# A decoder layer on one core: the first tile's output-weight rounding, gathers and mask loads moved, and 17 products of zeros added

## The reference

```python
x = layernorm(x + self_attn(x))           # 32 query heads, 8 key/value heads, width 16, causal, rotary
x = layernorm(x + cross_attn(x, ctx))     # 32 query heads, 8 key/value heads, width 128, mask, rotary at pos
x = layernorm(x + ffn(x))                 # x @ W.T + bias, kept where a cluster test says so

def self_attn(x):
    q, k, v = rope(x @ Wq), rope(x @ Wk), x @ Wv
    p = softmax(where(causal, q @ k.T / 4, -inf))
    return (p @ v) @ Wo
```

## Time and profile before

| what | value |
|---|---|
| median of 3 runs | 819.03 us (818.23 to 821.03) |
| profiled execution | 817.94 us |
| its span, first to last instruction | 816.0 us |
| PE, DVE, ACT, POOL busy | 758.6, 607.5, 317.6, 392.2 us |
| mean granted clock of TensorE | 0.989 |

### The profile page before, as it was taken

One profiled execution on the slowest core, in us unless ns is written; L12 is line 12 of the kernel. 1 busy time (PEld: TensorE's weight loads), 2 busy tenths in 40 slices (PEclk: granted clock), 3 DMA queues, 4 the chain that ended last, 5 costly groups with the idle time before them and its releaser, 6 DMA issues.

```text
span 816.0 us, 13861 instructions
## 1 busy us (share of the span) xinstructions
PE 758.6 (93%) x4800; PEld 649.0 (80%) x4800; DVE 607.5 (74%) x1165; ACT 317.6 (39%) x669; POOL 392.2 (48%) x369
## 2 busy tenths in 40 slices
PE   4689999989999999999999999999999999989984
PEld 3577777779878887888888888888888888877763
DVE  4778888877787676676677768677766776788767
ACT  4455555562433323343333334324233333333313
POOL 7566666664545544453544445444444644442102
PEclk9899999999999999999999999999999999999998
DMA  9500004012343232222232222242222232120002
GB/s 264 118 18 17 16 16 119 3 55 53 81 127 79 64 81 79 62 53 51 78 77 77 77 51 51 53 103 75 51 77 51 55 78 75 46 85 1 1 0 103
DMA packets 107875, 53.53 MB, mean 66 GB/s; under 512 B 80449, under 2 KB 96961, under 8 KB 107841
## 3 DMA queue, kind: packets, MB, share of 16 engines
q1 hardware_dynamic: 107008, 51.51, 24.7%
q10 hardware_dynamic: 576, 1.05, 0.4%
q0 software_dynamic: 256, 0.52, 0.2%
HBM read 32.62 MB, written 2.10 MB: 43 GB/s over the span
## 4 chain that ended last, share of the span: by engine, by line
PE 64%; DVE 19%; issue 6%; POOL 4%; ACT 2%; DMA 2%; SPq 2%; DVEq 0%; ACTq 0%; POOLq 0%
PE bank L723 17%; PE bank L658 17%; PE bank L484 10%; DVE arena_r L1512 5%; PE s_bank L737 3%; PE bank L534 2%; PE s_bank L739 2%; PE bank L707 2%; PE bank L558 2%; DVE small L1600 2%; DVE arena_f L1594 1%; PE s_bank L707 1%; ACT arena_r L979 1%; PE s_bank L558 1%; DMA arena_f<-in_L_attn_Wo 1%
## 5 line engine op out<-in xcount | busy, mean ns | idle before, releaser
L723 PE MATMUL bank<-arena_r 128*128 128x512 f32 x768 | 192.2, 399 | 0.9 <-DVE arena_r L1512 0.9
L979 ACT ACTIVATE arena_r<-bank 128x256 fp32r<-128x256 f32 (+2 forms) x249 | 105.1, 458 | 222.6 <-PE bank L690 88.6
L658 PE MATMUL bank<-arena_r 128*128 128x512 f32 x720 | 185.2, 400 | 2.2 <-POOL arena_r L1396 1.6
L723 PEld LDWEIGHTS bank<-arena_r 128*128 128x128 f32 x768 | 139.9, 189 | 28.2 <-DVE arena_r L1512 1.3
L658 PEld LDWEIGHTS bank<-arena_r 128*128 128x128 f32 x720 | 130.7, 188 | 31.5 <-POOL arena_r L1396 2.1
L484 PE MATMUL bank<-arena_r 128*128 128x256 f32 (+1 forms) x1056 | 146.7, 295 | 1.5 <-DVE arena_r L1512 0.6
L484 PEld LDWEIGHTS bank<-arena_r 128*128 128x128 f32 x1056 | 137.4, 191 | 9.0 <-DVE arena_r L1512 1.5
L1512 DVE TENSOR_TENSOR arena_r<-bank,arena_r 128x256 fp32r<-128x256 f32 (+2 forms) x217 | 99.9, 486 | 58.5 <-ACT arena_r L979 57.9
L979 ACT ACTIVATE arena_r<-arena_f 128x512 fp32r<-128x512 f32 (+2 forms) x178 | 104.4, 637 | 61.6 <-DMA arena_f<-arena_f 47.7
L1512 DVE TENSOR_TENSOR arena_r<-arena_f,arena_r 128x512 fp32r<-128x512 f32 (+1 forms) x100 | 92.9, 937 | 17.6 <-ACT arena_r L979 17.5
L1387 POOL TENSOR_TENSOR arena_f<-arena_f 128x512 f32<-128x512 f32 x30 | 39.2, 1306 | 114.2 <-DVE arena_f L1681 114.2
(11 more groups left out here) (153 smaller groups left out, 1169.9 us busy)
## 6 DMA issues: line engine op xcount, KB each, us to landing
arena_f<-arena_f SPq DMA_DIRECT2D x120, 128.0 KB, 2.5
arena_f<-in_L_xattn_Wo SPq DMA_DIRECT2D x8, 1024.0 KB, 5.6
arena_f<-in_L_xattn_Wq SPq DMA_DIRECT2D x14, 512.0 KB, 4.1
arena_f<-in_x SPq DMA_DIRECT2D x8, 256.0 KB, 2.8
arena_f<-in_x SPq DMA_DIRECT2D x1, 2048.0 KB, 15.5
arena_f<-in_L_xattn_Wk SPq DMA_DIRECT2D x8, 256.0 KB, 3.1
arena_f<-in_L_xattn_Wv SPq DMA_DIRECT2D x8, 256.0 KB, 3.3
arena_f<-in_ctx SPq DMA_DIRECT2D x8, 256.0 KB, 3.1
```

The lines of the kernel that those rows point to most:

```text
L658: mm = pe.matmul(BQ2[f][:], w2q_s[a][:, e, j, f, :], xT[b][:, e, tok], start=(e == 0 and n == 0), stop=(e == EC - 1 and n == 2))
L723: mm = pe.matmul(BO2[i][:], at2[a][:, h, i * P:(i + 1) * P], w2o_s[b][:, h, :], start=(h == 0 and n == 0), stop=(h == HG - 1 and n == 2))
L979: act.activation(dst, src, ACT.Copy).then_inc(done, 1)
```

## The change

Five edits. On SP, `next_x(1)` goes ahead of the W1o loads, and the two mask loads go behind `next_x(2)` and behind the four table copies. On ACT, the four roundings of W1o go from the start to tile 0, behind the last copy of `qk_stage(0)` and ahead of `expo(0, 0)`. On DVE, the four low pieces go from tile 0 to tile 1, two ahead of `masked_max(1, 1)` and two ahead of `masked_max(1, 3)`. On POOL, three of the eight gathers go behind the first tile's L1359. On PE, 17 products of a zeroed buffer into an unused bank are added: 5 ahead of `a_stage(0)`, 4 behind it, 8 ahead of `qk_stage(0)`; nothing reads them.

```diff
+            next_x(1)
             w1o_v = w1o.rearrange("(g h d) n -> g d h n", g=G1, h=HG)
             for g in range(G1):
                 sp.dma_start(w1out_raw[D1 * g:D1 * g + D1, :, :], w1o_v[g]).then_inc(d_w1o, 16)
-            next_x(1)
             sp.dma_start(res, x.rearrange("(t p) n -> p t n", p=P)).then_inc(d_res, 16)
-            for i in range(2):
+            def load_mask(i):
...
             next_x(2)
+            load_mask(0)
             sp.wait_ge(r_table, 2)
...
+            load_mask(1)
...
+            def warm(n):
+                for _ in range(n):
+                    pe.matmul(BO[:], vpad[0][:, 0, 0:P], vpad[0][:, 0, 0:512], start=True, stop=True)
...
+                if start:
+                    warm(8)
                 qk_stage(i, start)
...
+            pe.wait_ge(s_init, 1)
+            warm(5)
             pe.wait_ge(d_ident, 16)
             a_stage(0)
+            warm(4)
...
-            act.wait_ge(d_w1o, 16 * G1)
-            for h in range(HG):
-                copy(w1out[0][:, h, :], w1out_raw[:, h, :], s_w1oh)
...
                 if old:
                     at_high(v, not oldest)
+                else:
+                    act.wait_ge(d_w1o, 16 * G1)
+                    for h in range(HG):
+                        copy(w1out[0][:, h, :], w1out_raw[:, h, :], s_w1oh)
                 expo(i, 0)
...
-            for t in range(T):
+            for t in range(T - 3):
                 gather_rope(t)
...
+                if not old:
+                    for t in range(T - 3, T):
+                        gather_rope(t)
...
-                if not old:
-                    for h in range(HG):
-                        dve.wait_ge(s_w1oh, h + 1)
-                        low(w1out[1][:, h, :], w1out_raw[:, h, :], w1out[0][:, h, :], s_w1ol)
...
+                elif old:
+                    w1out_low(0)
+                    w1out_low(1)
                 masked_max(i, 1, not old)
...
+                elif old:
+                    w1out_low(2)
+                    w1out_low(3)
```

More of the change, by code:

```diff
@@ L1602, in total, with w1out_low @@
                 dve.reciprocal(sm1[u], sm1[u]).then_inc(s_rc, 1)
+            def w1out_low(h):
+                dve.wait_ge(s_w1oh, h + 1)
+                low(w1out[1][:, h, :], w1out_raw[:, h, :], w1out[0][:, h, :], s_w1ol)
             def tile_steps(i):
```

## The result

The changed kernel takes 826.79 us (median of 9 runs, 822.98 to 829.86) against 819.36 for the kernel before (9 runs). The ratio is 1.0088, 95% interval 1.0069 to 1.0107: slower by 7.4 us, 5.7 to 8.8. The direction was forecast; the size was not (823.7, range to 826.0), and the measured time lies outside the range. The profiled execution has a span of 824.1 us, 8.1 above the one before.

The account below looks back on a forecast made before the run. It took a chain through DVE's low pieces and `q_low` in tile 0, then `at_low(0)`, `wo_stage(0)`, `b_stage(2)` in tile 1, to bound the kernel. -5.9 + 1.8 + 7.0 + 1.8 = +4.7 us on 819.03 gave 823.7, range 818.3 to 826.0.

Parts of the forecast that it names:

- What bounds it, and the sign: Tile 1: `at_low(0)`, `wo_stage(0)`, `b_stage(2)` follow without a gap, PE has no slack; slower given 0.60.
- Gain of tile 0: Tile 0: `qk_stage(0)` starts at 18.3, not 22.75, and `masked_max(0, 0)` at 22.6, not 28.52; gain 5.9 us.
- The gathers' wait: Tile 0: `table_turn` on PE waits for three late gathers, landing at 26.3; cost 1.8 us, bounds 0.8 and 3.6.
- the prediction's own rule: Tile 0: for no cost, `table_turn` must start by 24.5, early enough for `masked_max(0, 2)` 4.15 us after the first.
- The stand of `wo_stage(0)`: Tile 1: PE waits for DVE's last low pieces, slowed by POOL; cost 7.0 us, bounds 4.8 and 7.4.
- Its clock: Tile 1: PE's half clock behind the wait slows `wo_stage(0)` and `b_stage(2)`; cost 1.8 us, bounds 0 and 2.3.
- The sum: Whole kernel: -5.9 + 1.8 + 7.0 + 1.8 = +4.7 us, span 820.7, median 823.7.
- Rival 3: Tile 0: gathers land at 28.1, or half clock takes 1.4 off the gain; +6.1 to +6.5, about 825.3; chance 0.11.
- The loads of x and the masks, ACT's roundings: Moved loads on SP and W1o roundings on ACT cost nothing; 0.5 if ACT were late by one rounding.
- The signs: Profile: `qk_stage(0)` near 18.3 at clock 1.0, `table_turn` waits 2 to 4 us, `wo_stage(0)` 5 to 7.5, then half clock.
- The 1.2 GHz of `b_stage(0)` before: Tile 0, kernel before: `b_stage(0)` took 5.29 us against 3.00 for the same shape, so ran at 1.2 GHz.

Follow-up runs that it names:

- experiment 1: Changed kernel, but DVE makes all four low pieces of W1o in tile 1 ahead of `x_low(2)`; 817.31 us, ratio 0.9986 to the kernel before.
- experiment 7: Kernel before with only the W1o edits on ACT (roundings) and DVE (low pieces in tile 1); 825.66 us, ratio 1.0088 to the kernel before.
- experiment 3: Changed kernel with W1o low pieces ahead of `x_low(2)` and `table_turn` behind `s_stage(0, (2, 3))`; 815.08 us, ratio 0.9949 to the kernel before.
- experiment 5: Changed kernel plus 24 products of 512 columns on PE ahead of tile 1's `wo_stage(0)`; 824.81 us, ratio 1.0070 to the kernel before.
- experiment 9: Changed kernel, but all eight gathers ahead of POOL's first addition; 824.40 us, ratio 1.0083 to the kernel before.
- Experiment 10: Changed kernel plus 14 more products of zeros on PE ahead of `table_turn`; 824.32 us, ratio 1.0071 to the kernel before.
- experiment 6: Changed kernel, but W1o's low pieces formed from a PSUM bank, not the raw weights (true low part left out); 823.87 us, ratio 1.0059 to the kernel before.
- experiment 4: Changed kernel without the 17 products of zeros; 825.71 us, ratio 1.0076 to the kernel before.
- experiment 8: Changed kernel with W1o low pieces ahead of `x_low(2)` and `table_turn` behind `b_stage(1)` in tile 1; 813.28 us, ratio 0.9935 to the kernel before.

## Why the prediction failed in size

**What bounds it, and the sign.** Right. The chain through `at_low(0)`, `wo_stage(0)`, `b_stage(2)` had no slack, and the wait for the low pieces came through whole (experiments 1 and 7).

**Gain of tile 0.** Predicted 5.9, measured 5.6, and the agreement is in part luck. W1v landed 1.8 us earlier, so `rope_q(0)` was done early and POOL's addition, now held by its fifth gather, started at 13.49 instead of 14.65; `qk_stage(0)` started at 17.27 instead of 18.3. Against that, the clock fell near 17.9 in this execution, after PE had stood from 15.4 to 17.3, which cost the 1.4 that the zeros were to buy. I had them ending at 17.4, right ahead of the transposes; they began and ended 2 us earlier. In four traces it held behind a gap of 1.2 to 1.9 us (experiments 1, 3, 5 and 9), and the gain was 6.8 in experiment 1.

**The gathers' wait.** This is the step that failed: "Cost 1.8 us, bounds 0.8 and 3.6", measured 4.0. What failed in it is not the wait. The chain through the last gather reads:

```profile
21.02 5.52 DMA arena_f<-in_c_rope,pos_i
26.55 0.04 issue
26.59 1.12 PE bank L611 x4
27.71 0.85 PE s_bank L611 x4
```

It landed at 26.55, and I had 26.3. That was luck: I had it issued at 22.5 and landing 3.8 us later; it was issued at 21.02 and took 5.5 us, like those under load. By the prediction's own rule `table_turn` had to start by 22.93 + 4.15 - 2.26 = 24.8, so this wait alone costs the predicted 1.8. The other 2.2 us are the clock, which this step put at nothing. I priced `table_turn` at 1.1 and the scores at 1.16 us, both at full clock, although PE stood still for 3.8 us ahead of them. At half clock they took 2.0 and 1.9, which is 1.7 at `masked_max(0, 2)`; and `b_stage(1)` took 5.15, which ended its slack (`rope_q(1)` waited 0.41 us for PE) and made the last 0.5. Experiment 10's trace shows it (its time alone is inconclusive): with the clock at 1.0 the same step costs 2.3, the wait and no more. I had reckoned with the clock for the stand of tile 1 and not for this one, so even the upper bound was no bound. How much of the half clock the stand itself makes stays open: in experiment 9 it came without one, behind a later start of tile 0, at a cost of 0.8.

The failure doesn't hang on this one execution. By the prediction the lead at `masked_max(1, 0)` was to be 4.1 us (5.9 - 1.8). In the five traces with the gathers in this place it was 0.4 to 1.6.

**The stand of `wo_stage(0)`.** Predicted 7.0, measured 6.9, of which 2.26 go with POOL's operations (experiment 6; predicted 2.2). Mechanism and size were right. The upper bound was summed wrongly: three pieces that each let one operation go ahead are 4.8 + 3 x 1.04 = 7.9, not 7.4; the measured step lies under both. **Its clock.** Predicted 1.8, measured 2.3, the far end: the clock rose at 62.3, 4.9 us behind the restart and not 3.6.

**The sum.** +4.7 predicted, +7.6 at `rope_q(2)`: 2.2 of the error are the clock behind the gathers' wait, 0.5 the clock in tile 1, 0.3 the front, and the stand gives 0.1 back. Rival 3 had the late gathers at 28.1, or tile 0 at half clock. The gathers landed at 26.55; tile 0 was at half clock here, but that was offset by the earlier start. Its price was reached, and passed, by the clock behind the gathers.

**The loads of x and the masks, ACT's roundings.** Costed at nothing. ACT's roundings fitted (22.35 to 24.56, `expo` at 25.53). The loads were not tried alone. Experiments 7 and 9, which differ by them and the zeros, are 0.4 us apart by ratio, with intervals that leave room for about 3 us, so this cost is not shown to be nothing.

**The signs.** Of the signs named for being right, the waits ahead of `table_turn` (3.81) and `wo_stage(0)` (5.83), the half clock behind the second and the long pairs (2.13 and 2.65) came. `qk_stage(0)` at granted clock 1.0 didn't in this trace. The 1.2 GHz of `b_stage(0)` before was read from its length (5.29 us for what takes 3.00) alone: the profile gives 1.00 as granted clock for that stretch, so its rows don't settle it.

## What to carry to other kernels

An instruction moved off a busy place has a deadline: look up who waits for it, and put it ahead of that wait, where its own engine stands idle and the engine that it would get in the way of (here POOL) does too. Here four instructions cost 1.0% in the wrong place, and in the right one PE waited for them no longer than before. When a reordering makes an early stage faster, ask which later step waits for something that didn't move (the gathers' landing), since the gain ends there. Price every new stand of TensorE twice, once as the wait and once as the half clock on what follows, down to the first stage with slack. And where a trace is read to 1 us, read several executions: the clock in `qk_stage(0)` came out either way for the same order of work.

## What the runs showed of the hardware

The half clock lasted longer than in the kernel before (26.4 - 19.6 = 6.8 us): in the changed kernel 10.2 us twice (24.7 to 35.0, 52.0 to 62.3), although PE was working from 26.59 and 57.36 on, that is for the last 8.4 and 4.9 us of it. In experiment 5 it lasted 3.4 us (53.2 to 56.6), with PE filled throughout. It had fallen there 0.8 us into a dense run of products, behind a gap of 1.4 us and 1.0 us of scores.

The same work does not always end at the same clock. Behind the eight zeros and a stand of 1.9 us, the granted clock in `qk_stage(0)` fell at 17.9 in the changed kernel's trace and near 19.0 in experiment 6, and stayed at 1.0 in experiments 1 and 5. Work begun at the end of a stand, or in one, may come too late to save the clock, but the traces give no rule for it.

Executions of kernels with the same loads ahead of it saw W1v land between 6.3 us (experiment 4) and 8.6 us (experiment 8) after its issue. Everything in tile 0 starts from that load, but it explains at most a part of the spread of the runs (822.98 to 829.86): the stretch behind `rope_q(2)` alone differed by 4.5 us from trace to trace. What makes it differ was not looked for.
